# Adding precomputed parts by an identity product in PSUM, and one restarting scan for the places

## What is computed

```python
# second graph layer (x is normalised first; u_expanded is the same row for all nodes)
combined = jnp.concatenate([x, edge_attr_agg, u_expanded], axis=1)   # 256 + 64 + 128
h = jax.nn.relu(combined @ W1 + b1)                                  # 512 hidden units
x = x + (h @ W2 + b2)
# mixture of experts: 8 experts, the best two per node
gate_scores = x_norm @ Wg.T + bg
topk_scores, topk_idx = jax.lax.top_k(gate_scores, 2)
topk_probs = softmax(topk_scores)
out = sum over e of combine[..., e] * (relu(x_norm @ W1[e].T + b1[e]) @ W2[e].T + b2[e])
```

## Time and profile before

| | us |
|---|---|
| median of 3 runs | 3171.64 (3166.49 to 3179.81) |
| the profiled execution | 3179.43 |
| its span | 3177.7 |
| second dense part, from its first product to the first transpose of the blocks | 2228.5 to 2405.7 |
| wide blocks, from there to | 3013.4 |
| PE busy in the span | 2488.2 (78%) |

### The profile page before, as it was taken

How to read it: one execution, slowest core, us unless ns; L and a number is a source line. 1 busy time by engine, 2 the same in 40 slices (tenths; PEclk the granted TensorE clock), 3 DMA queues, 4 the chain that set the end, 5 groups by cost and what they waited for, 6 DMA issues and landing times. The chain is left out here.

```text
span 3177.7 us, 48200 instructions
## 1 busy us (share of the span) xinstructions
PE 2488.2 (78%) x11785; PEld 1961.3 (62%) x11786; DVE 1430.2 (45%) x3684; ACT 951.0 (30%) x2290; POOL 1837.5 (58%) x1901
## 2 busy tenths in 40 slices
PE   0555665666667589999998890919998999999998
PEld 0334444544445456666665890919567888888898
DVE  6322223878873233343343890819585222222222
ACT  4766333333333233443433000000452111111122
POOL 4777777777777677777777767772155222322222
PEclk9878777788888789999999995969899999999999
DMA  6333334333333321212222761725476444444464
GB/s 216 98 104 104 104 104 125 104 104 105 104 103 104 92 66 63 72 63 73 73 72 82 198 175 51 211 86 134 158 245 196 115 108 117 116 118 104 115 181 136
DMA packets 218733, 373.32 MB, mean 117 GB/s; under 512 B 49205, under 2 KB 147358, under 8 KB 217631
## 3 DMA queue, kind: packets, MB, share of 16 engines
q0 software_dynamic: 82928, 157.51, 19.2%
q1 hardware_dynamic: 77916, 154.55, 14.8%
q10 hardware_dynamic: 57812, 60.35, 6.8%
HBM read 290.56 MB, written 81.71 MB: 117 GB/s over the span
## 5 line engine op out<-in xcount | busy, mean ns | idle before, releaser
L920 POOL DMA_INDIRECT sorted_edges<-arena x768 | 744.3, 969 | 303.2 <-issue 225.0
L343 POOL DMA_INDIRECT arena<-xn_rows,arena x784 | 749.6, 956 | 249.2 <-issue 228.1
L673 PE MATMUL psum<-arena 128*128 x1984 | 614.6, 475 | 343.8 <-ACT arena L408 323.2
L673 PEld LDWEIGHTS psum<-arena 128*128 128x128 f32 x1984 | 461.1, 240 | 497.3 <-issue 415.3
L408 ACT ACTIVATE arena<-arena 128x256 f32<-128x256 f32 x784 | 333.9, 496 | 567.5 <-DMA arena<-xn_rows,arena 567.5
L1205 PE MATMUL psum<-arena,acc 128*65 128x128 f32 x2720 | 316.5, 278 | 161.3 <-DVE arena L1373 161.2
L1205 PEld LDWEIGHTS psum<-arena,acc 128*65 128x65 f32 x2720 | 301.4, 140 | 176.2 <-DVE arena L1373 166.1
L1373 DVE SCALAR_TENSOR_TENSOR arena<-psum,acc 128x512 f32<-128x512 f32 x340 | 252.7, 744 | 168.2 <-DMA acc<-sorted_edges 150.5
L1804 PE MATMUL psum<-arena,xr 128*128 x1344 | 299.1, 381 | 2.0 <-DVE xr L2034 2.0
L1791 PE MATMUL psum<-xr 128*128 128x256 f32 x1344 | 299.4, 381 | 0.9 <-DVE xr L2028 0.9
L575 DVE TENSOR_TENSOR acc<-acc,psum 128x256 f32 x248 | 103.2, 416 | 405.8 <-PE psum L673 405.5
(11 more groups left out here) (320 smaller groups left out, 3203.9 us busy)
## 6 DMA issues: line engine op xcount, KB each, us to landing
xr<-in_f_W_dram SPq DMA_DIRECT2D x63, 1024.0 KB, 5.1
acc<-sorted_edges ACTq DMA_DIRECT2D x340, 132.0 KB
arena<-in_attr_dram SPq DMA_DIRECT2D x28, 924.0 KB, 5.2
arena<-xn_rows,arena POOLq DMA_INDIRECT x784, 2.8
sorted_edges<-arena POOLq DMA_INDIRECT x784
arena<-hidden_parts SPq DMA_DIRECT2D x7, 1792.0 KB, 8.4
arena<-dispatched SPq DMA_DIRECT2D x42, 265.0 KB, 2.8
arena<-in_f_W_dram SPq DMA_DIRECT2D x8, 1024.0 KB, 12.0
```

The lines of the kernel that those rows point to most:

```text
L343: pool.indirect_dma_start(out=rows[:, c, :], out_offset=None, in_=xn_d, in_offset=bass.IndirectOffsetOnAxis(ap=idx[:, c:c + 1], axis=0)).t ...
L673: last = nc.tensor.matmul(psum[:, bank(u), 0:D], hot[:, u, c, :], rows[:, ds(slots[k] + c, 1), :].squeeze(1), start=c == 0, stop=c == RUN - 1)
L920: pool.indirect_dma_start(out=edges_d, out_offset=bass.IndirectOffsetOnAxis(ap=pos_i[:, c:c + 1], axis=0), in_=stage[:, q % 2, c % SC, :], ...
```

## The change

The eight DVE additions per group go. Each product q of `hidden(g)` is followed on PE by a second product into the same bank, of the 128 x 128 identity with the columns of `hx5`, so that the sum of both stands in PSUM. ACT's relu reads the bank and writes `h5`. The semaphore `s_hadd` goes with the additions: SP and the bank waits of PE use `s_h5` (the products) and `s_hc5` (the relus). PE now waits for the load of `hx5` ahead of a group's first product, and a node tile k below 4 for the relu of product k + 4.

In `places` the eight scans become one scan over 56 numbers, laid out expert by tile, which multiplies the running sum by 0 at the first tile of each expert and by 1 elsewhere, and one addition of the bases. The multipliers are set once by two memsets.

```diff
-            both6 = sb("both6", [P, G, NX], f32, ph6)
+            both6 = sb("both6", [P, NX, G], f32, ph6)
+            again6 = sb("again6", [P, NX, G], f32, ph6)
...
-                        sp.wait_ge(s_hadd, g * 8 + 8)
+                        sp.wait_ge(s_h5, PHASES * 4 + g * 8 + 8)
...
-                    sp.wait_ge(s_hadd, NG * 8)
+                    sp.wait_ge(s_h5, PHASES * 4 + NG * 8)
...
-                            act.wait_ge(s_hadd, g * 8 + q + 1)
-                            nc.scalar.activation(h5[:, m, c0:c1], h5[:, m, c0:c1], ACT.Relu,
+                            act.wait_ge(s_h5, PHASES * 4 + g * 8 + q + 1)
+                            nc.scalar.activation(h5[:, m, c0:c1], psum[:, 4 + q % 4, 0:c1 - c0], ACT.Relu,
...
                         pe.wait_ge(s_x3, g * G)
+                        pe.wait_ge(s_hx, g * 16 + 16)
                         for q in range(8):
                             m, (c0, c1) = q % 4, HALVES[q // 4]
                             if q >= 4:
-                                pe.wait_ge(s_hadd, g * 8 + q - 3)
+                                pe.wait_ge(s_hc5, PHASES * 4 + g * 8 + q - 3)
-                            nc.tensor.matmul(psum[:, 4 + q % 4, 0:c1 - c0], gw1e[:, m, :], mean, start=True, stop=True).then_inc(s_h5, 1)
+                            nc.tensor.matmul(psum[:, 4 + q % 4, 0:c1 - c0], gw1e[:, m, :], mean, start=True, stop=False)
+                            nc.tensor.matmul(psum[:, 4 + q % 4, 0:c1 - c0], ident[:, :], hx5[:, m, c0:c1], start=False, stop=True).then_inc(s_h5, 1)
...
-                        if k in (0, 4):
-                            pe.wait_ge(s_hc5, PHASES * 4 + g * 8 + k + 4)
-                        if k == 0:
-                            pe.wait_ge(s_hadd, g * 8 + 8)
-                        if k >= 4:
+                        if k < 4:
+                            pe.wait_ge(s_hc5, PHASES * 4 + g * 8 + k + 5)
+                        else:
                             pe.wait_ge(s_x3, g * G + k - 3)
...
+                    own.add(nc.vector.memset(again6[:, :, :], 1.0))
+                    own.sync()
+                    own.add(nc.vector.memset(again6[:, :, 0:1], 0.0))
...
-                    def add_parts(g):
-                        dve.wait_ge(s_hx, g * 16 + 16)
-                        for q in range(8):
-                            m, (c0, c1) = q % 4, HALVES[q // 4]
-                            dve.wait_ge(s_h5, PHASES * 4 + g * 8 + q + 1)
-                            nc.vector.tensor_tensor(h5[:, m, c0:c1], psum[:, 4 + q % 4, 0:c1 - c0], hx5[:, m, c0:c1], ALU.add).then_inc(s_hadd, 1)
...
-                        for e in range(NX):
-                            own.add(nc.vector.tensor_tensor_scan(pos6[:, :, e], both6[:, :, e], both6[:, :, e], bas6[:, e:e + 1], ALU.add, ALU.bypass))
+                        own.add(nc.vector.tensor_tensor_scan(pos6 as (e t), again6 as (e t), both6 as (e t), 0.0, ALU.mult, ALU.add))
+                        own.sync()
+                        own.add(nc.vector.tensor_tensor(pos6[:, :, :], pos6[:, :, :], bas6[:, :].unsqueeze(2).to_broadcast([P, NX, G]), ALU.add))
```

More of the change, by code:

```diff
@@ L788, in build @@
             gt5 = {n: sb("gt5_" + n, [P, G, NX], f32, ph6) for n in ("g", "eq", "sc", "o1", "g2", "eq2", "sc2", "o2")}
-            both6 = sb("both6", [P, G, NX], f32, ph6)
+            both6 = sb("both6", [P, NX, G], f32, ph6)
+            again6 = sb("again6", [P, NX, G], f32, ph6)
             cnt6 = sb("cnt6", [P, NX], f32, ph6)
             bas6 = sb("bas6", [P, NX], f32, ph6)
-            pos6 = sb("pos6", [P, G, NX], f32, ph6)
+            pos6 = sb("pos6", [P, NX, G], f32, ph6)
             sel6 = sb("sel6", [P, 2, G, NX], f32, ph6)
@@ L1909, in gates @@
                         own.add(nc.vector.tensor_tensor(gt5["sc2"][:, :, :], gt5["o2"][:, :, :], wide(g5["w2"][:, :], NX), ALU.mult))
-                        own.add(nc.vector.tensor_tensor(both6[:, :, :], gt5["o1"][:, :, :], gt5["o2"][:, :, :], ALU.add))
+                        own.add(nc.vector.tensor_tensor(both6[:, :, :].rearrange("p e t -> p t e"), gt5["o1"][:, :, :], gt5["o2"][:, :, :], ALU.add))
                         own.sync()
-                        nc.vector.tensor_reduce(cnt6[:, :], both6[:, :, :].rearrange("p t e -> p e t"), AX.X, ALU.add).then_inc(s_n7, 1)
+                        nc.vector.tensor_reduce(cnt6[:, :], both6[:, :, :], AX.X, ALU.add).then_inc(s_n7, 1)
                         own.add(nc.vector.tensor_tensor(xs6[:, g % 3, :, D + 1:ED], gt5["sc"][:, :, :], gt5["sc2"][:, :, :], ALU.add))
@@ L1918, in places @@
                         own.add(nc.vector.tensor_tensor(run6[:, :], psum[:, 7 if g == NG - 1 else 3, 0:NX], run6[:, :], ALU.add))
-                        for e in range(NX):
-                            own.add(nc.vector.tensor_tensor_scan(pos6[:, :, e], both6[:, :, e], both6[:, :, e], bas6[:, e:e + 1], ALU.add, ALU.bypass))
+                        own.add(nc.vector.tensor_tensor_scan(pos6[:, :, :].rearrange("p e t -> p (e t)"), again6[:, :, :].rearrange("p e t -> p (e t)"),
+                                                             both6[:, :, :].rearrange("p e t -> p (e t)"), 0.0, ALU.mult, ALU.add))
+                        own.sync()
+                        own.add(nc.vector.tensor_tensor(pos6[:, :, :], pos6[:, :, :], bas6[:, :].unsqueeze(2).to_broadcast([P, NX, G]), ALU.add))
                         own.sync()
                         for n, of in enumerate(("o1", "o2")):
-                            own.add(nc.vector.tensor_tensor(sel6[:, n, :, :], gt5[of][:, :, :], pos6[:, :, :], ALU.mult))
+                            own.add(nc.vector.tensor_tensor(sel6[:, n, :, :], gt5[of][:, :, :], pos6[:, :, :].rearrange("p e t -> p t e"), ALU.mult))
                         own.sync()
@@ L1931, in _ @@
                     node_columns(0)
-                    add_parts(0)
                     node_columns(1)
@@ L2049, in _ @@
                         deviations(g - 1)
-                        add_parts(g)
                         if g == EARLY + 1:
```

1 line of the change is left out of this document (removed).

## The result

| | before | after |
|---|---|---|
| median of 4 runs each, us | 3172.29 (3166.49 to 3179.81) | 3230.86 (3227.11 to 3236.02) |
| profiled execution, its span, us | 3179.43, 3177.7 | 3228.87, 3227.2 |
| a group of the second dense part, us | 21.89 | 30.64 |

The ratio is 1.0182 [1.0164, 1.0200], 58.6 us slower. The forecast had the sign and the place right and the size wrong: 32.9 us, and the range ended at 3216. A busy-time table would hardly give it away: PE is busy 2547.8 us, 79% of the span, where it was 78%.

What follows compares the result with a forecast made beforehand. PE was taken as the bound of the second dense part, ACT close behind. Terms 5.9 + 22.8 + 2.1 + 4.2 - 2.1 = 32.9 us, on a median of 3171.6, gave 3204.5; range 3190 to 3216.

Steps and rivals of the forecast that it cites:

- Their weight loads lie under the products, as those of the present ones do.: Eight identity products per group: weight loads hidden, so they cost 6.02 us of PE, 5.71 on the path.
- PE has no longer pause than before, so I keep the times.: Group 0: clock falls at 2241.92 and rises at 2252.04 as before, nodes start at 2258.0 instead of 2252.15, +5.9 us.
- The bound of +11.8: Group 0, upper bound: cost in us were the clock to rise only at the nodes.
- The rival on the clock: Denser PE may keep 2.4 GHz in group 0 and through the pause ahead of the first block: 3196 us, chance 0.07.
- The wait of 0.3 us ahead of the nodes: Usual group, before the change: PE stands still about 0.3 us between reciprocals and node products.
- The identity's full price: Each group's identity products: two MATMULs each, 0.43 us per 512 columns, 6.02 us a group.
- Half price: Rival: identity products cost half, like a transpose, 3.0 us less a group; 3184 us, chance 0.05.
- room on PE: Rival: ACT's chain bounds the group and identity products hide beside it; 3166 us, not slower, chance 0.04.
- The relu from PSUM: ACT's eight relus per group: 0.57 us each, at 0.9 still shorter than PE's pair; cost taken as 0.
- The 3.65 us: Group 5's extra length, from the first table after DVE's additions, comes back: 5.71 - 3.65 = 2.06 us added.
- The load ahead of the blocks: SP's load of the first blocks' rows after group 6 lands at its median: -2.1 us; otherwise +1.1.
- `hx5` was never late: Rival: the load of `hx5` holds a group's first product; 3226 us, chance 0.04.

Runs made afterwards that it cites:

- e2_rows64: The changed kernel with identity products of 64 rows too, leaving out the precomputed part of half the hidden units; 3201.21 us in one run.
- e3_pad128: The changed kernel with attribute products padded to 128 rows, the upper 64 of their weights zeros; 3202.02 us, ratio 1.0085.
- e5_scan_only: The kernel before with the one scan of the change and nothing else of it; 3175.78 us over ten runs, ratio 1.0001.
- e7_split_table: The kernel before with the one scan, and the first table laid out in two pieces, in groups 5 and 6; 3177.43 us, ratio 0.9994.
- e1_grouped: The changed kernel with products reordered: in each half four of the attributes, then four of the identity; 3208.36 us, ratio 1.0108.
- e10_pad_later: The changed kernel with attribute products padded to 128 rows from group 1 on, group 0 keeping 64 rows; 3219.13 us, ratio 1.0127.
- e4_no_identity: The changed kernel without the identity products, so the precomputed parts are left out; 3199.18 us in one run.
- e9_reordered: The kernel before with one scan, additions before statistics, relus before scaled rows, waits per bank, first table in two pieces; 3178.24 us, ratio 1.0007.

## Why the forecast missed its size

Of the 30.5 us by which the stage outgrew the sum (63.4 against 32.9), two steps account for nearly all, the first for some 22, the second for some 8.6.

*"Their weight loads lie under the products, as those of the present ones do."* This failed. Products of 128 rows had been priced by a stretch where all products have 128 rows, products of 64 by one where all have 64. Both prices were right, as e2_rows64 and e3_pad128 show; no row had the two alternating. What was missing is 15 changes of 0.195 us, 2.9 us a group: 17.6 us of the 17.8 by which groups 1 to 6 outgrew the sum. In group 0, at 1.2 GHz, the same 15 changes cost 0.28 us each, 4.2 together.

*"PE has no longer pause than before, so I keep the times."* This failed too. The prediction let the clock rise with 5.97 us of work still ahead of the nodes; it rose only at the nodes. The 13.70 us of work take 27.4 at 1.2 GHz, and with the 4.2 of the changes that makes 31.6; measured are 31.53, where the forecast had 18.75. The bound of +11.8, the clock rising only at the nodes, was of the right kind, but it kept the first 2.67 us at 2.4 GHz and had no changes of rows in it. What held the clock down is shown in part: with alternating products it stayed low, with 128 rows throughout group 0 cost +3.2, and between the changes and the 64 rows the runs don't decide. The times that the prediction kept were also those of one execution: e5_scan_only and e7_split_table, where PE has the same work as before, took 15.42 us from first product to first node instead of 12.90. The rival on the clock had looked to the other side only, that a denser PE keeps 2.4 GHz.

Three small readings are off, and none decides. The wait of 0.3 us ahead of the nodes was half that: the nodes start 1.65 us behind the reciprocals where PE waits for nothing, 1.81 before, and the sum had 1.50. The clock shares 0.92 and 0.96 were read as if the rest stood still; at 1.2 GHz for the rest they put the fall at 2241.84 and the rise at 2252.08. And 5.05 - 2.8 is 2.25, where the sum has 2.1.

The other steps held:

- The identity's full price: 6.0 us a group, as MATMULs of 0.43 us (e3_pad128). Half price is out, and so is room on PE, since a group of e3_pad128 grew by nearly all of it, 5.81 us. The sentence of the Trainium skill on which that rival rested ("Perfetto Trace Analysis", "Identifying the Most-Contended Engine") names the share of weight loads beside MFU, the work done as a share of the peak. As far as weight loads go, the trace is against it once more: the share of PEld fell to 16.11 of 30 us in group 2 while PE was busy 29.97 of them.
- The relu from PSUM: not shown before, taken at 0.57 us, and at 0.9 still under cover. By form it took 0.68 us for 512 columns, and PE waits for it nowhere in groups 1 to 6:

```profile
L1639 ACT ACTIVATE arena<-psum,arena 128x512 f32<-128x512 f32 x28 | 17.7, 676 | 20.1 <-PE psum L1743 20.1
```

- Group 5: its products start at 2362.25 and those of group 6 at 2392.89, 30.64 us, no longer than its neighbours. The 3.65 us came back.
- The load ahead of the blocks. The forecast took the long issue of `fb2` for a full queue and not for its own length. The record bears that out. SP's timeline now has it at 0.34 us instead of 8.64. It starts 14.28 us behind the issue ahead of it on the queue (`fb1`, the experts' first bias, L1491) instead of 5.97, and it ends 14.62 us behind that issue where it ended 14.61:

```profile
2438.76 0.34 SPq L1493 DMA_DIRECT2D acc<-in_f_b_dram  x1
...
2452.48 1.46 SPq L1502 DMA_DIRECT2D arena<-dispatched  x2
```

  The first transpose starts at 2455.31, 2.83 us behind that issue instead of 5.05: 2.2 us back where 2.1 were forecast.
- `hx5` was never late: PE waits ahead of no group for it. The scan was worth 0 in groups 1 to 4.

## What to carry to other kernels

Before adding a product between others, look at the number of rows of its neighbours: a price taken from a stretch of equal products doesn't hold for an alternating one, and padding the smaller operand with zeros (27 us slower than before instead of 59) or grouping equal ones (33 us) was cheaper here than changing at each product. An engine off the path may still serve the path by emptying banks; leave its work out as an experiment before counting it as free to move. And a PE that is busy in every microsecond can stay at 1.2 GHz, and pauses can be too short to be written as waits, so read the granted clock and compare starts of like instructions, not busy shares. A stretch whose clock differs between executions of the same work needs more than one profile before its times go into a sum.

## What the runs showed of the hardware

- A change between 64 and 128 rows in the stationary operand from one product to the next delayed the next by 0.193 to 0.196 us at 2.4 GHz, with its weight loads not begun while the product ahead streams (PEld idle 0.76 us); in e2_rows64 one such change, into products of 64 stationary columns, cost nothing. The Trainium skill, page "TensorE: Matmul & The Clock Gate", section "Step-by-step: what each phase is for", says that loads are pulled ahead where their row groups don't conflict or where they go to the background buffer, and that their time doesn't depend on the number of rows. The trace agrees on the second point: in e1_grouped a single load took 0.19 us with 64 rows and with 128. On the first it agrees for equal rows, and where the rows changed no load was pulled ahead; which of the two conditions fails there was not shown.
- At 1.2 GHz an alternating product of 512 columns takes 2.00 us (2225.39 to 2227.39), twice 0.86 and 0.28 more. In all three profiled executions with alternating products in group 0 (the changed kernel twice, e10_pad_later) the clock stayed at 1.2 GHz from the first product until about the first node, 31.5 to 31.8 us, with PE busy throughout. In four kernels with 64 rows and no change of rows (e4_no_identity, e5_scan_only, e7_split_table, e9_reordered) it stayed there through all of group 0's products, 12.31 us, with PE busy throughout as well.
- One DMA issue, that of `fb2`, took between 0.34 and 9.23 us in the 13 profiled executions, the same transfer with the same instruction. It began 5.2 to 14.3 us behind the issue of `fb1` on the same queue and ended 13.0 to 15.2 us behind it: that fits an issue that waits for what stands ahead of it.
